# Attention over a long context on one core: value products of two key tiles one behind the other in every second step

## The chip, the cores and the metric

One core of one Trainium2 chip runs the whole program. The metric is the device time of one execution in microseconds (us), the median of three executions of the kernel before: 3383.43 us.

## The reference, cut to what matters

`x` is 32 examples of 64 latent rows of width 256; `ctx_512` is 32 examples of 1601 context rows of width 64. Six blocks are added to `x` one after the other: a small cross attention, a self attention, a quantised MLP, then the cross attention over the whole context (the block that the change touches), a self attention and a mixture of experts.

```
q_big = rope((hidden_q @ Wq.T) per head @ w_kc_q)        # 16 heads, width 192
kv_r  = rope(kv_c)                                       # 1601 x 64, shared by the heads
q_r   = einsum('bshq,hqr->bhsr', q_big, W_qr)
k_r   = einsum('bld,hdr->bhlr', kv_r, W_kr)
scores = einsum('bhsr,bhlr->bhsl', q_r, k_r)
attn  = softmax(scores, axis=-1)
ctx_c = einsum('bhsl,bld->bhsd', attn, kv_r)
out   = einsum('bhsd,hkd->bhsk', ctx_c, w_kc_kv) ... @ Wo.T
```

## The kernel before

The block is `context_attention`. The per-head weights have been folded ahead of it, so that for every example (a **batch** here, n = 0 to 31) the scores are products of the turned context keys with 1024 query columns (16 heads of 64 rows), held as two halves p = 0, 1 of 512 columns. Two batches share one tile of 128 rows of `x`: the even one (e = 0) comes first, then the odd one (e = 1). The 16 tiles are the repeats of the work; most of them run in a loop over t.

The 1601 keys lie in NKT = 13 tiles of 128 (the last has 65). A batch has 13 **steps**, kt = 0 to 12. The order on each engine is written out by hand in its `batch` function, and semaphores tie the engines together. In step kt:

- TensorE (PE in the profile) makes the scores of the *next* key tile, `scores(n, t, e, kt + 1, p)` (L813 and L814, two products that are added, into the PSUM banks `st[0]` and `st[1]`), one half in each of the first two thirds of the step. In the last third it makes the value products of *this* key tile, `values(n, e, kt)` (L825): the 128x64 tile of `kv` against the 512 exponentials of each half, the halves into partitions 0 to 63 and 64 to 127 of the one bank `av`, where all 13 key tiles are summed. The trace shows the two products of a `values` as four matmuls.
- ScalarE (ACT) makes the exponentials, `exps(n, kt)` (L965): one of 128x512 for each half, from `st[p]` into `prob`, a ring of RING = 4 buffers, and a fifth for key tile 12. A buffer is free again once the value products and the sum over keys (POOL) of four tiles before are done.
- GpSimd (POOL) adds the exponentials up over the key tiles, `add(n, kt)` (L685).
- VectorE (DVE) takes row maxima of the *next* batch: TensorE makes 16 **pieces** of plain scores a batch (`max_scores`, L790, into the two `mx` banks in turn), VectorE reduces each (`reduce_max`, L1062). A piece's products wait until VectorE is through with the piece two before it. The function `pieces` spreads the 16 over the thirds: in an even batch from the second third of step 1 to the end of step 6, in an odd one from step 3 to step 9.

`scores(kt + 2, p)` needs `st[p]` back, so it waits for the exponential of kt + 1, half p. `values(kt)` waits for both exponentials of kt, and in step 0 for `summed` (ScalarE's copy of the last batch's `av`). Other work lies on TensorE between the thirds:

- after step 0 `denominators(n - 1)` (L837), once GpSimd's last addition of the batch before is done; later, in steps 2 and 3, VectorE inverts them in two halves (`invert`, L1075) and scales the heads (L1080), in its program behind the pieces of step 2 and of step 3;
- after step 5 of an even batch `out(t - 1)` (L844), after step 6 `turn_x` (L737), which waits for all 16 pieces;
- in steps 7 to 12 of an even batch the queries of the next tile (L747, L761); in steps 7 to 10 of every batch the turning of keys (L728);
- in step 11 `max_rows` (L799), 16 small products, which ScalarE copies before the next batch's first scores can start; they stand ahead of that step's value products.

The lines that set the order of scores and values are these:

```
for kt in range(NKT):
    for third in range(3):
        if third == 2:
            values(n, e, kt)
        elif kt + 1 < NKT:
            scores(n, t, e, kt + 1, third)
```

Of the kernel before, what the change touches and what calls it, by code (L numbers as in the profile page):

```python
# [403 lines left out]
NKT = -(-SK // P)  # L404
# [77 lines left out]
def context_attention(nc, sb, pb, sem, a, x_all, const, wbig, mw, wvo):  # L482
# [91 lines left out]
    def nk(kt):  # L574
        return min(P, SK - kt * P)
# [13 lines left out]
    def pieces(e, kt, third):  # L589

        start, end = (9, 3 * NEGATE_AT + 3) if e else (4, 3 * QUERIES_AT)
        first = lambda k: min(max(0, -(-(k - start) * PIECES // (end - start))), PIECES)
        return range(first(3 * kt + third), first(3 * kt + third + 1))

    def slot(kt):

        return kt % RING if kt < NKT - 1 else RING
# [13 lines left out]
    def is_first(n):  # L611
        return isinstance(n, int) and n == 0

    with nc.Block() as block:
# [105 lines left out]
        def _(pe):  # L720
            def turn_keys(n, r):

                if r == 0:
                    pe.wait_ge(s_kl, n + 1)
                else:
                    pe.wait_ge(s_kp, KROUNDS * n + r)
                for kt in range(4 * r, min(4 * r + 4, NKT)):
                    last = pe.transpose(misc[:, kt % 4 * P:(kt % 4 + 1) * P], khl[:, kt, :, :], ident[:, :])  # L728
                last.then_inc(s_kt, 1)

            def turn_x(t):
                pe.wait_ge(s_xn, t + 1)

                if not is_first(t):
                    pe.wait_ge(s_mr, 2 * t * PIECES)
                for c in range(DC):
                    last = pe.transpose(mx[0][:, 0, c * P:(c + 1) * P], xn[:, c * P:(c + 1) * P], ident[:, :])  # L737
                last.then_inc(s_xT, 1)
# [27 lines left out]
            def queries(t, j):  # L766

                if 2 <= j < CP + 2:
                    effective(t, j - 2)
                if j < CP:  # L770
                    big(t, j)

            def max_scores(t, n, e, i):
                b = i % 2
                if i == 0:

                    pe.wait_ge(s_kp, KROUNDS * (n + 1))
                    if e == 0:
                        pe.wait_ge(s_q1a, 2 * t + 2)
                        pe.wait_ge(s_q2a, 2 * t + 2)  # L780
                    else:
                        pe.wait_ge(s_q1b, t + 1)
                        pe.wait_ge(s_q2b, t + 1)
                if not (is_first(n) and i < 2):

                    pe.wait_ge(s_mr, n * PIECES + max(i - 1, 0))
                q = q1[e][:, :, :, :].rearrange("p e j s -> p (e j s)")[:, (i // 2) * P:(i // 2 + 1) * P]
                for h in range(2):
                    lo = (2 * b + h) * KQ
                    last = pe.matmul(mx[b][:, h, 0:KQ], q, kp[e][:, lo:lo + KQ], start=True, stop=True)  # L790
                last.then_inc(s_mx, 1)

            def max_rows(n, p):

                if p == 0:
                    pe.wait_ge(s_nm, n + 1)
                for i in range(4):
                    for part, (w, lo) in enumerate(((nmh, True), (nml, False))):
                        last = pe.matmul(mx[p][0:1, 0, i * P:(i + 1) * P], w[:, 4 * p + i:4 * p + i + 1], identb[:, :],  # L799
                                         start=(part == 0), stop=(part == 1))  # L800
                last.then_inc(s_row, 1)

            def scores(n, t, e, kt, p):
                keys = slice(kt * P, kt * P + nk(kt))
                g = 2 * kt + p
                if not (is_first(n) and g < 2):

                    pe.wait_ge(s_exp, n * 2 * NKT + g - 1)
                if g == 0:

                    pe.wait_ge(s_rowk, 2 * n + 2)
                    pe.wait_ge(s_kd[e], 32 * t + 32)
                pe.matmul(st[p][0:nk(kt), :], k1[e][:, keys], q1[e][:, p, :, :], start=True, stop=False)  # L813
                pe.matmul(st[p][0:nk(kt), :], k2[e][:, keys], q2[e][:, p, :, :], start=False, stop=True)\  # L814
                    .then_inc(s_st, 1)

            def values(n, e, kt):
                pe.wait_ge(s_exp, n * 2 * NKT + 2 * kt + 2)
                if kt == 0:

                    pe.wait_ge(s_kv, n + 1)
                    if not is_first(n):
                        pe.wait_ge(s_avk, n)
                for p in range(2):
                    last = pe.matmul(av[DCX * p:DCX * p + DCX, :], kv[e][0:nk(kt), kt, :],  # L825
                                     prob[slot(kt)][0:nk(kt), p, :], start=(kt == 0), stop=(kt == NKT - 1))
                last.then_inc(s_av, 1)

            def denominators(n):

                pe.wait_ge(s_acc, (n + 1) * NSUM)
                if isinstance(n, int) and n > 0:

                    pe.wait_ge(*((s_hd, n) if n % 2 else (s_x, n // 2)))
                pe.wait_ge(s_rowk, min(2 * n + 4, 2 * B) if isinstance(n, int) else 2 * n + 4)
                for p in range(2):
                    last = pe.matmul(misc[DCX * p:DCX * p + DCX, :], ones[:, :], acc[:, p, :], start=True, stop=True)  # L837
                last.then_inc(s_sum, 1)

            def out(t):  # L840

                pe.wait_ge(s_hd, 2 * t + 2)
                for j in range(CP):
                    last = pe.matmul(misc[:, 0:D], heads[:, j, :, :], wvo[:, j, :],  # L844
                                     start=(j == 0), stop=(j == CP - 1))
                last.then_inc(s_out, 1)
# [18 lines left out]
            def batch(n, t, e, more, next, far):  # L865
                for kt in range(NKT):
                    for third in range(3):
                        if third == 2:
                            values(n, e, kt)
                        elif kt + 1 < NKT:  # L870
                            scores(n, t, e, kt + 1, third)
                        elif next:
                            scores(n + 1, t + e, 1 - e, 0, third)
                        if more and e == 0 and third < 2 and 0 <= kt - QUERIES_AT <= CP // 2:
                            queries(t + 1, 2 * (kt - QUERIES_AT) + third)
                        if next:
                            for i in pieces(e, kt, third):
                                max_scores(t + e, n + 1, 1 - e, i)
                            if kt == ROWS_AT and third == 1:
                                max_rows(n + 1, 0)  # L880
                                max_rows(n + 1, 1)
                    if kt == QUERIES_AT - 1 and more and e == 0:
                        turn_x(t + 1)
                    if kt == 0 and not is_first(n):
                        denominators(n - 1)
                    if kt == OUT_AT and e == 0 and not is_first(n):
                        out(t - 1)
                    if 0 <= kt - TURN_AT < KROUNDS and more:
                        if kt == TURN_AT and not is_first(n):

                            if e == 0:
                                pe.wait_ge(s_x, t)
                            else:
                                pe.wait_ge(s_hd, n)
                        turn_keys(n + 2, kt - TURN_AT)

            batches(pe, before, batch)
            denominators(B - 1)
            out(NT - 1)
# [990 lines left out]
```

## Time and profile before

| what | value |
|---|---|
| median of 3 executions | 3383.43 us (3383.25 to 3397.73) |
| profiled execution, its own time | 3396.48 us |
| its span | 3394.7 us |
| mean granted TensorE clock over the span | 0.928 of full speed |
| busy TensorE / VectorE / ScalarE / GpSimd | 86% / 47% / 37% / 36% of the span |

The span is what lies between the first and the last instruction on the core. The profiled execution is one of several, and it took 13 us more than the median. The context attention runs from about 757 us to 2530 us of the span. Busy TensorE means that a matmul was in flight, at either clock.

### The profile page before, as it was taken

The numbers are of one execution on the slowest core, as the hardware profiler recorded it, in microseconds if no ns is written. First come the engines' busy times: TensorE is split into PE (matmuls) and PEld (weight loads), VectorE is DVE, ScalarE is ACT, GpSimd is POOL, SyncE is SP. The second block draws the span as 40 slices with busy tenths as digits, with TensorE's granted clock in tenths as the row PEclk, the third lists the DMA queues.
The fourth block names the chain that finished last, engine by engine and source line by source line (L and its number), as shares of the span: only waits on it lengthen the run. The fifth ranks groups of instructions, "written<-read, shape, count | busy, mean of one in ns | idle before, by whom it ended". The sixth has DMA issues, their size and how long they took to land. (4 is left out here: it accounts for less than half of the span.)

```text
span 3394.7 us, 49700 instructions
## 1 busy us (share of the span) xinstructions
PE 2916.8 (86%) x17527; PEld 1787.8 (53%) x17528; DVE 1579.7 (47%) x2705; ACT 1260.5 (37%) x2514; POOL 1232.9 (36%) x656
## 2 busy tenths in 40 slices
PE   5867734659999999999999999999977789999998
PEld 3544422535545554555455554555434467777776
DVE  3444567533554455444544464445526643333232
ACT  3433412114344334433443344344424333333332
POOL 0000000035676567656765676557650000000000
PEclk9778866679999999999999999999988899999999
DMA  1000030011111011110111111111011000000000
GB/s 40 0 17 0 0 121 0 0 58 40 36 49 39 25 35 49 39 35 33 41 39 35 39 35 39 35 39 35 30 72 77 0 1 0 0 0 0 0 0 25
DMA packets 26434, 98.27 MB, mean 29 GB/s; under 512 B 3536, under 2 KB 8272, under 8 KB 24976
## 3 DMA queue, kind: packets, MB, share of 16 engines
q1 hardware_dynamic: 24720, 94.02, 8.4%
q10 hardware_dynamic: 1664, 3.58, 0.3%
q8 instruction: 32, 0.52, 0.1%
q14 instruction: 18, 0.15, 0.0%
HBM read 55.97 MB, written 2.10 MB: 17 GB/s over the span
## 5 line engine op out<-in xcount | busy, mean ns | idle before, releaser
L685 POOL TENSOR_TENSOR cx_acc<-cx_acc,cx_prob 128x1024 f32<-128x1024 f32 (+1 forms) x352 | 834.7, 2371 | 509.0 <-ACT cx_prob L965 501.5
L965 ACT ACTIVATE cx_prob<-cx_st 128x512 f32<-128x512 f32 (+1 forms) x832 | 477.5, 596 | 595.2 <-PE cx_st L814 577.5
L1062 DVE TENSOR_REDUCE cx_mhalf<-cx_mx 128x1 f32<-128x804 f32 x512 | 486.1, 988 | 219.2 <-PE cx_mx L790 219.1
L825 PE MATMUL cx_av<-cx_prob,cx_kv 128*64 128x512 f32 (+1 forms) x1664 | 456.8, 628 | 0.0
L813 PE MATMUL cx_st<-cx_q,cx_k 128*128 128x512 f32 (+1 forms) x832 | 369.0, 444 | 50.0 <-ACT cx_prob L965 49.4
L1528 PE MATMUL moe_gu<-moe_wgu,moe_xnT 128*128 128x352 f32 x1280 | 397.6, 462 | 0.0
L790 PE MATMUL cx_mx<-cx_kp,cx_q 128*128 128x402 f32 x1024 | 304.0, 380 | 62.6 <-DVE cx_mhalf L1062 59.2
L814 PE MATMUL cx_st<-cx_q,cx_k 128*128 128x512 f32 (+1 forms) x832 | 332.4, 400 | 0.0
L1528 PEld LDWEIGHTS moe_gu<-moe_wgu,moe_xnT 128*128 128x128 f32 x1280 | 241.5, 191 | 124.1 <-issue 6.2
L790 PEld LDWEIGHTS cx_mx<-cx_kp,cx_q 128*128 128x128 f32 x1024 | 174.7, 193 | 248.5 <-DVE cx_mhalf L1062 186.0
L1043 DVE TENSOR_TENSOR cx_turn<-cx_mx,cx_tab 128x384 f32<-128x384 f32 x256 | 130.9, 553 | 358.3 <-PE cx_mx L747 358.3
L1663 DVE SCALAR_TENSOR_TENSOR moe_hid<-moe_silu,moe_coef,moe_gu 128x176 f32<-128x176 f32 x320 | 127.0, 397 | 350.2 <-ACT moe_silu L1591 348.1
L813 PEld LDWEIGHTS cx_st<-cx_q,cx_k 128*128 128x128 f32 (+1 forms) x832 | 157.8, 190 | 204.2 <-ACT cx_prob L965 143.7
L1591 ACT ACTIVATE moe_silu<-moe_gu 128x176 f32<-128x176 f32 x320 | 101.6, 318 | 370.8 <-PE moe_gu L1528 370.8
L1493 POOL TENSOR_TENSOR moe_rstd<-moe_mv,minus_half 128x1 f32<-128x1 f32 x16 | 8.8, 549 | 614.2 <-DVE moe_mv L1628 614.2
L1551 PE MATMUL moe_acc<-moe_wd,moe_hidT 128*128 128x256 f32 (+1 forms) x896 | 216.1, 382 | 0.0
L747 PE MATMUL cx_mx<-cx_xnT,cx_wbig 128*128 128x128 f32 x1536 | 204.7, 283 | 0.5 <-ACT cx_xnT L928 0.5
L761 PE MATMUL cx_mx<-cx_turn,cx_mw 128*64 128x128 f32 (+1 forms) x2048 | 197.0, 296 | 0.0
L747 PEld LDWEIGHTS cx_mx<-cx_xnT,cx_wbig 128*128 128x128 f32 x1536 | 183.2, 192 | 25.0 <-issue 16.5
L924 ACT CAST cx_kp<-cx_misc 128x512 fp32r<-128x512 f32 (+1 forms) x128 | 64.8, 507 | 324.2 <-PE cx_misc L728 324.2
L1551 PEld LDWEIGHTS moe_acc<-moe_wd,moe_hidT 128*128 128x128 f32 (+1 forms) x896 | 160.2, 190 | 21.9 <-issue 5.3
L814 PEld LDWEIGHTS cx_st<-cx_q,cx_k 128*128 128x128 f32 (+1 forms) x832 | 156.8, 188 | 7.5
(209 smaller groups left out, 3701.3 us busy)
## 6 DMA issues: line engine op xcount, KB each, us to landing
cx_k<-cx_kp SPq DMA_DIRECT2D x32, 804.0 KB, 4.0
cx_ctx<-in_cx_ctxN SPq DMA_DIRECT2D x32, 416.0 KB, 3.2
cx_ctxr<-in_cx_ctxrN SPq DMA_DIRECT2D x32, 416.0 KB, 3.9
cx_k<-cx_kp SPq DMA_DIRECT2D x32, 402.0 KB, 5.2
moe_wgu<-in_moe_wgu SPq DMA_DIRECT2D x5, 1408.0 KB, 14.6
moe_wd<-in_moe_wd SPq DMA_DIRECT2D x4, 896.0 KB, 24.6
x_all<-in_x SPq DMA_DIRECT2D x1, 2048.0 KB, 4.2
cx_wq<-in_cx_wq SPq DMA_DIRECT2D x1, 2048.0 KB, 11.8
```

What stands on the lines that cost most here:

```text
L685: pool.tensor_tensor(acc[rows, :, :], sofar, prob[slot(kt)][rows, :, :], ALU.add).then_inc(s_acc, 1)
L747: last = pe.matmul(mx[j % 2][:, 0, tile * P:(tile + 1) * P], wbig[:, c, j, tile * P:(tile + 1) * P], xnT[:, c, :], start=(c == 0), stop=(c ...
L761: last = pe.matmul(mx[j // 4][DCX * e:DCX * e + DCX, 1, at:at + P], mw[rows, j, cs, tile, :], turn[j % 2][rows, cs, tile, :, :], start=(cs ...
L790: last = pe.matmul(mx[b][:, h, 0:KQ], q, kp[e][:, lo:lo + KQ], start=True, stop=True)
L813: pe.matmul(st[p][0:nk(kt), :], k1[e][:, keys], q1[e][:, p, :, :], start=True, stop=False)
L814: pe.matmul(st[p][0:nk(kt), :], k2[e][:, keys], q2[e][:, p, :, :], start=False, stop=True)\
L825: last = pe.matmul(av[DCX * p:DCX * p + DCX, :], kv[e][0:nk(kt), kt, :], prob[slot(kt)][0:nk(kt), p, :], start=(kt == 0), stop=(kt == NKT ...
L965: act.activation(prob[slot(kt)][rows, p, :], st[p][rows, :], ACT.Exp).then_inc(s_exp, 1)
L1043: last = dve.tensor_tensor(turn[j % 2][:, cs, :, :, :], q, tab[:, cs, :, :].unsqueeze(2).broadcast_to([P, 3, 2, S]), ALU.mult)
L1062: dve.tensor_reduce(mhalf[:, i // 2, i % 2:i % 2 + 1], mx[i % 2][:, :, 0:KQ], AX.XY, ALU.max)\
L1528: last = pe.matmul(gu[i][:, 0:2 * FE], xnT[g][:, c, :], wgu[:, e, c, :], start=(c == 0), stop=(c == DC - 1))
L1551: last = pe.matmul(acc[:, 0:D], hidT[q % 2][0:n, k % 4, :], wd[0:n, k, :], start=(k == 0), stop=(k == NFC - 1))
```

## The change

`values` is no longer made in steps 0, 2, 4, 6, 8 and 10. In each odd step the value products of the key tile before and of this one stand one behind the other; step 12, the last, makes those of key tile 12 alone, as before. No product is added or left out; scores, pieces and all else stay where they were.

```
                 for kt in range(NKT):
                     for third in range(3):
                         if third == 2:
-                            values(n, e, kt)
+                            if kt % 2 == 1:
+                                values(n, e, kt - 1)
+                            if kt % 2 == 1 or kt == NKT - 1:
+                                values(n, e, kt)
                         elif kt + 1 < NKT:
                             scores(n, t, e, kt + 1, third)
```

TensorE, the start of an odd batch in the loop (steps 0 and 1; REGISTER_ALU and ISA rows compute addresses and waits). Before:

```order
L825 MATMUL cx_av<-cx_prob,cx_kv 64x512 x2
L831 REGISTER_ALU
L835 ISA
L837 MATMUL cx_misc<-cx_acc,cx_ones 64x512 x2
L808 REGISTER_ALU
L813 MATMUL cx_st<-cx_q,cx_k 128x512
L814 MATMUL cx_st<-cx_q,cx_k 128x512
L808 REGISTER_ALU
L813 MATMUL cx_st<-cx_q,cx_k 128x512
L814 MATMUL cx_st<-cx_q,cx_k 128x512
L825 MATMUL cx_av<-cx_prob,cx_kv 64x512 x2
```

With the change:

```order
L831 REGISTER_ALU
L835 ISA
L837 MATMUL cx_misc<-cx_acc,cx_ones 64x512 x2
L808 REGISTER_ALU
L813 MATMUL cx_st<-cx_q,cx_k 128x512
L814 MATMUL cx_st<-cx_q,cx_k 128x512
L808 REGISTER_ALU
L813 MATMUL cx_st<-cx_q,cx_k 128x512
L814 MATMUL cx_st<-cx_q,cx_k 128x512
L821 REGISTER_ALU
L825 MATMUL cx_av<-cx_prob,cx_kv 64x512 x4
```

The value products of key tile 0 have left their place ahead of the denominators (L837) and stand with those of key tile 1, behind the scores of key tile 2.

TensorE, even batch, the end of step 4 and the start of step 5 (the pieces are the L790 rows). Before:

```order
L813 MATMUL cx_st<-cx_q,cx_k 128x512
L814 MATMUL cx_st<-cx_q,cx_k 128x512
L786 REGISTER_ALU
L790 MATMUL cx_mx<-cx_kp,cx_q 128x402 x2
L825 MATMUL cx_av<-cx_prob,cx_kv 64x512 x2
L786 REGISTER_ALU
L790 MATMUL cx_mx<-cx_kp,cx_q 128x402 x2
```

With the change:

```order
L813 MATMUL cx_st<-cx_q,cx_k 128x512
L814 MATMUL cx_st<-cx_q,cx_k 128x512
L786 REGISTER_ALU
L790 MATMUL cx_mx<-cx_kp,cx_q 128x402 x2
L786 REGISTER_ALU
L790 MATMUL cx_mx<-cx_kp,cx_q 128x402 x2
```

The two pieces now follow each other directly; the value products that stood between them come behind the pieces of step 5.

## Rows read from the trace of the kernel before

**Rows 1.** Windows: the context attention, then one tile slow in clock, one not
```profile
core 0: us, PE busy (x) PEld busy (x) DVE busy (x) ACT busy (x) POOL busy (x), PEclk, DMA share, GB/s
757.00:2530.00 1773.00, 1642.49 (x9019) 921.68 (x9018) 865.50 (x1096) 738.27 (x1341) 1143.24 (x516) 0.98 0.11 36
...
1392.06:1504.14 112.08, 104.35 (x582) 58.91 (x581) 55.78 (x71) 46.67 (x86) 72.71 (x34) 0.98 0.11 37
1504.14:1614.69 110.55, 102.84 (x581) 58.23 (x580) 55.78 (x71) 46.67 (x86) 72.69 (x34) 1.00 0.12 38
```

**Rows 2.** Waits of TensorE, 800 to 2480 us: total, times, longest
```profile
PE cx_mx L790 <- DVE cx_mhalf L1062: 53.7, 45, 1.7
PE cx_st L813 <- ACT cx_prob L965: 48.7, 61, 1.8
```

**Rows 3.** The page's part 5, exponentials and reductions: busy, mean ns, idle before
```profile
L965 ACT ACTIVATE cx_prob<-cx_st 128x512 f32<-128x512 f32 (+1 forms) x832 | 477.5, 596 | 595.2 <-PE cx_st L814 577.5
L1062 DVE TENSOR_REDUCE cx_mhalf<-cx_mx 128x1 f32<-128x804 f32 x512 | 486.1, 988 | 219.2 <-PE cx_mx L790 219.1
```

**Rows 4.** Timeline of TensorE around one value step: start, us, [idle before]
```profile
1415.32 0.53 PE L790 MATMUL cx_mx<-cx_kp,cx_q 128*128 128x402 f32 x2
1415.69 0.39 PE L813 MATMUL cx_st<-cx_q,cx_k 128*128 128x512 f32 x1
...
1416.15 0.53 PE L790 MATMUL cx_mx<-cx_kp,cx_q 128*128 128x402 f32 x2
1416.60 1.08 PE L825 MATMUL cx_av<-cx_prob,cx_kv 128*64 128x512 f32 x4
1417.61 0.64 PE L790 MATMUL cx_mx<-cx_kp,cx_q 128*128 128x402 f32 x2
1418.09 0.39 PE L813 MATMUL cx_st<-cx_q,cx_k 128*128 128x512 f32 x1
```

**Rows 5.** Timeline of TensorE, odd batch, steps 0 to 2
```profile
1506.27 1.08 PE L825 MATMUL cx_av<-cx_prob,cx_kv 128*64 128x512 f32 x4
1507.18 1.03 PE L837 MATMUL cx_misc<-cx_acc,cx_ones 128*64 128x512 f32 x4
1508.68 0.50 PE L813 MATMUL cx_st<-cx_q,cx_k 128*128 128x512 f32 x1 [0.47 <-ACT cx_prob L965]
...
1509.83 1.08 PE L825 MATMUL cx_av<-cx_prob,cx_kv 128*64 128x512 f32 x4
1512.72 0.50 PE L813 MATMUL cx_st<-cx_q,cx_k 128*128 128x512 f32 x1 [1.81 <-ACT cx_prob L965]
```

**Rows 6.** Timeline of TensorE, even batch, steps 4 to 6
```profile
1452.40 1.08 PE L825 MATMUL cx_av<-cx_prob,cx_kv 128*64 128x512 f32 x4
1455.14 0.64 PE L790 MATMUL cx_mx<-cx_kp,cx_q 128*128 128x402 f32 x2 [1.66 <-DVE cx_mhalf L1062]
...
1458.99 3.61 PE L844 MATMUL cx_misc<-cx_wvo,cx_heads 128*128 128x256 f32 x16
...
1465.42 0.44 PE L737 MATMUL cx_mx<-ident,cx_xn 128*128 128x128 f32 x2 [0.16 <-DVE cx_mhalf L1062]
```

**Rows 7.** Timeline of TensorE, odd batch, steps 4 and 5
```profile
1519.62 1.08 PE L825 MATMUL cx_av<-cx_prob,cx_kv 128*64 128x512 f32 x4
...
1522.78 0.64 PE L790 MATMUL cx_mx<-cx_kp,cx_q 128*128 128x402 f32 x2 [1.05 <-DVE cx_mhalf L1062]
```

**Rows 8.** Timeline of VectorE in the same steps of that batch
```profile
1519.34 1.76 DVE L1075 RECIPROCAL cx_misc<-cx_misc 128x256 f32<-128x256 f32 x1
1521.13 0.69 DVE L1080 TENSOR_TENSOR cx_heads<-cx_summed,cx_misc 128x512 f32<-128x512 f32 x1
```

**Rows 9.** Timeline of TensorE, where the even batch begins
```profile
1434.29 0.50 PE L813 MATMUL cx_st<-cx_q,cx_k 128*128 128x512 f32 x1 [0.48 <-ACT cx_prob L965]
...
1439.02 1.08 PE L837 MATMUL cx_misc<-cx_acc,cx_ones 128*64 128x512 f32 x4 [0.38 <-POOL cx_acc L685]
```

**Rows 10.** Windows: the same work of an odd batch in two tiles
```profile
1401.80:1405.34 3.54, 3.54 (x10) 1.75 (x10) 0.07 (x1) 1.07 (x3) 3.46 (x2) 0.52 0.00 0
1513.88:1515.83 1.95, 1.95 (x10) 1.05 (x10) 0.07 (x1) 0.85 (x3) 1.87 (x2) 1.00 0.00 0
```

## The prediction

> **What bounds the kernel now.** I read the windows first, then the waits, then the timelines of one tile, engine by engine. The change touches 757 to 2530 us alone. There TensorE is busy for 1642 of 1773 us, GpSimd for 1143, VectorE for 866, ScalarE for 738 [rows 1]: TensorE sets the time wherever it doesn't wait. The tiles repeat: of the 14 in the middle, 11 take 112.1 us at a granted clock of 0.98 and three take 110.5 us at 1.00. TensorE's waits are few and always in the same places: 53.7 us for VectorE ahead of pieces, 48.7 us for ScalarE ahead of scores [rows 2]. These places decide. A value product that leaves a step where TensorE then waits leaves for nothing, since the wait grows by as much; where it lands, it costs its full time.
>
> **What the change saves.** The value products use the array in two halves of 64 columns (the form 128\*64), all around them uses it whole (128\*128). Each change of form shows in the starts [rows 4]: from a piece to the scores behind it 0.37 us; from a piece to value products 0.45; from value products to the next piece 1.01, where from value products to denominators, of the same form, it is 0.91 [rows 5]; and the first piece behind value products takes 0.48 instead of 0.37. So a visit to the narrow form costs 0.08 + 0.10 + 0.10 = about 0.28 us of TensorE besides the 0.91 us of its work. A batch loses five visits (steps 2, 4, 6, 8, 10; in step 0 the denominators keep the form), 160 in all, and at most 160 x 0.28 = 45 us.
>
> The page "TensorEngine Tiling (Array Packing)" of the Trainium skill, section on tiling modes, says that changing the mode drains the array; by this rule alone the sum would be those 45 us, with no price for the waits. The rows agree that a change costs something.
>
> **What it costs, step by step.** I move the value products in the timelines with the durations above: 0.91 us for a second `values` behind a first, 0.60 us for an exponential, about 0.95 to 0.99 us for a reduction [rows 3]. V4 stands for the value products of key tile 4.
>
> *Even batch.*
> - V0: TensorE waits 0.38 us for GpSimd's last addition ahead of the denominators [rows 9]. Without V0 that wait is 1.3 us; V0 lands in step 1: **+0.91**.
> - V2: VectorE falls behind. It needs three reductions (2.9 us) a step, TensorE's step without values gives only 0.93 for scores and 1.1 for pieces, so its pieces wait 0.9 us; what is left of the gain is given back when V2 lands: **about 0**, with VectorE's chain through both reciprocals 0.9 us late from V0.
> - V4: the wait of 1.66 us ahead of the first piece behind it [rows 6] is VectorE's (reciprocal, heads, reduction). V4's leaving makes it 2.6 to 2.9 us; its landing in step 5 delays `out`: **+0.91**.
> - V6: `turn_x` waits 0.16 us for the last reductions [rows 6], which end when they end; V6 lands in step 7, where queries keep TensorE full: **+0.91**.
> - V8: full TensorE on both sides: **-0.28**.
> - V10: full ahead, and behind step 11 stands a wait of 0.48 us for ScalarE's chain from `max_rows` to the exponential [rows 9], which V10 now fills: -0.28 - 0.5, **about -0.8**.
>
> Sum: 3 x 0.91 - 0.28 - 0.8 = about +1.6 us; drawn through the timelines I get +1.5.
>
> *Odd batch.*
> - V0: ScalarE holds the scores of step 1 (0.47 us of wait) and of step 2 (1.81) [rows 5]: V0 leaves one wait and fills half of the other: **0**, and the 1.81 becomes 0.9.
> - V2: without V2 the scores of key tile 4 wait for the exponential of 3 (score to score at least 0.9 + 0.6 us): leaves 0.6 to 0.7, lands 0.91, a switch less: **about +0.2**.
> - V4: the first piece of step 5 waits 1.05 us for VectorE's second reciprocal (1.76 us), the heads (0.69) and a reduction [rows 7, 8]. The wait becomes 2.2 us, V4 lands behind it: **+0.8**.
> - V6, V8: two pieces a step leave VectorE time. V6 gains its 0.28 and loses it to a piece's wait, V8 gains 0.28 and takes up a wait for keys: **-0.3** together.
> - V10: as in the even batch, but TensorE stands idle sooner, for the exponentials: **-0.2**; and what has become late is partly hidden where the next batch waits for GpSimd's additions: **-0.2**.
>
> Sum: about +0.3 us. A tile therefore gains 1.5 + 0.25 = +1.75 us; over 15 tiles with pieces **+26 us**. The ends: if each landing costs only 0.6 us (part of the new waits vanishing, as V2's), a tile is at 5 x 0.6 less 2.5 saved, or 0; if the savings of steps 8 and 10 don't come, it is at +3.3, or 50 us. Scalar and vector work, DMAs and GpSimd's additions are the same and keep their order. The ring of exponentials doesn't bind: exponential 4 waits for V0, now in step 1, and is asked for at the end of step 3.
>
> **The clock.** In 11 of the 14 tiles TensorE's clock falls from 2.4 to 1.2 GHz right behind the wait of 1.81 us, and never behind those of 1.66 or 1.05 us. The same work then takes 3.54 us instead of 1.95 [rows 10], and the tile 1.55 us more [rows 1]. The change takes this wait to 0.9 us: 11 x 1.55 = 17 us saved if the dips go. It makes two longer ones, 2.6 to 2.9 us (even, step 5) and 2.2 us (odd, step 5). If each brings the dip as often as the 1.81 did, with 1.2 us of it on the path since VectorE is behind there anyway, that is 2 x 11 x 1.2 = 26 us more. Net +9; with dips in every tile at both places 15 x 2 x 1.3 - 17 = +22; with none -17. I take **+12**.
>
> The page "TensorE: Matmul & The Clock Gate" of the Trainium skill (its table on why this matters) warns against idle gaps between bursts of matmuls, since they bring the clock back to half; by this rule the two new waits speak against the change, and the sum with that term is +38 us, without it +26. The trace agrees for the wait of 1.81 us.
>
> **Sum.** +26 + 12 = +38 us. The profiled execution took 3396.5 us and would take 3434; it stands 13 us above the median, perhaps by its dips, and I lay the sum on the median: 3383.4 + 38 = **3421 us**.
>
> **Rivals.**
> - *The switches are worth it (faster).* The waits on VectorE and ScalarE don't grow, because what TensorE does earlier brings the pieces and scores earlier by as much: the mechanism is the mode change, its place every even step, its price 0.28 us, and it decides once fewer than two of the five landings a tile cost their 0.91. With all 160: 3383 - 45 = 3338 us. With the landings at half price (5 x 0.45 = 2.3 us) and ten visits at 0.28 (2.8 us): -0.5 us a tile, and the clock's -17: about 3359 us. For it: TensorE is 93% busy. Against: all five landings leave a place that shows a wait [rows 5 to 7, 9]. Chance 0.10.
> - *A draw.* The landings cost as I say, but more of it is hidden at batch ends by ScalarE and GpSimd, and the clock dips fall away without new ones: 26 - 17 + little = 3383 to 3400 us. Chance 0.22.
> - *VectorE's bound in full.* Every even step with pieces loses 0.9 us against VectorE's reductions, and both new waits bring a dip in every tile: 50 + 22 = +72, 3455 us. For it: reductions take 2.9 us where TensorE's work for the same pieces now takes 2.0. Against: the paired products leave VectorE 2 us to catch up, and the odd batch has only two pieces in most steps. Chance 0.15.
> - *Nothing changes in kind:* the trace of after would show the same waits. It can't be: the order of instructions differs as shown. Chance 0.
>
> My forecast (3400 to 3445 us) has 0.53.
>
> **How the numbers follow.** 0.5% is 17 us, about what can be told from no change here. Slower by more, over 3400: the forecast and the third rival, 0.68. Faster by more, under 3366: 0.10. Within: 0.22. The range for 8 in 10 reaches down over the draw, to 3380, and up to 3452, short of the third rival's end.
>
> **What would show it.** In the new profile: value products in runs of eight matmuls, the second four 0.91 us behind the first; 160 fewer changes of form; the wait at the denominators of the even batch at 1.3 us; the wait in step 5 of the even batch above 2.4 us and that of the odd one at 2.2; the 1.81 us wait at 0.9 and no dip behind it; dips behind the two in step 5; tile periods of 113 to 116 us. I am wrong if the tile period falls below 110.5 us, if the waits for VectorE stay near 54 us in sum, or if the clock stays at 1.00 in most tiles.

## The result and the profile after

| | before | with the change |
|---|---|---|
| median | 3384.62 us (3383.25 to 3397.73, 4 runs) | 3454.18 us (3439.20 to 3459.22, 4 runs) |
| profiled execution, its span | 3396.48, 3394.7 us | 3459.22, 3457.4 us |
| mean granted TensorE clock | 0.928 | 0.917 |

The change made the kernel slower: the ratio is 1.0189, with a 95% interval of 1.0158 to 1.0220. The direction and the places were as forecast, but the loss was larger: the medians differ by 70 us, the means of the executions (from which the ratio comes) by 64, where I had said 38. The median of 3454 us lies above my forecast of 3400 to 3445 us, and 2 us above the 3452 to which the range for 8 in 10 reached; 1.0189 of the 3383.4 us on which I had laid the sum is 3447.

Busy time in the profile of the change (part 1 of the page), and its costliest groups that the change touches (part 5). The lines below `values` have moved by three (L965 is L968, L1062 is L1065).

```profile
PE 2920.2 (84%) x17527; PEld 1824.7 (53%) x17528; DVE 1597.9 (46%) x2705; ACT 1259.2 (36%) x2514; POOL 1230.2 (36%) x656
...
L825 PE MATMUL cx_av<-cx_prob,cx_kv 128*64 128x512 f32 (+1 forms) x1664 | 425.0, 630 | 0.0
L790 PE MATMUL cx_mx<-cx_kp,cx_q 128*128 128x402 f32 x1024 | 319.5, 397 | 89.7 <-DVE cx_mhalf L1065 86.2
```

The instruction counts are the same, and TensorE is busy for as long as before (2920 us against 2917) in a span that is 63 us longer. The value products themselves (L825) are busy for 425 us instead of 457, for less of each visit is overhead. The pieces (L790) have become longer one by one (397 ns against 380). A slower clock would do that: the rows below show a piece at 1.04 us instead of 0.64.

The waits of TensorE in the context attention of the change, 800 to 2540 us, to be read as [rows 2]: total, times, longest.

```profile
PE cx_mx L790 <- DVE cx_mhalf L1065: 80.8, 60, 2.7
PE cx_st L813 <- ACT cx_prob L968: 44.1, 60, 1.3
PE cx_misc L837 <- POOL cx_acc L685: 26.6, 14, 1.9
PE cx_mx L737 <- DVE cx_mhalf L1065: 17.6, 15, 1.3
```

The wait for VectorE ahead of pieces has grown from 53.7 to 80.8 us, and two waits that were small are now large: for GpSimd ahead of the denominators (0.38 us each before [rows 9], now 1.9) and for VectorE ahead of `turn_x` (0.16 before [rows 6], now 1.2). The longest wait for ScalarE has gone from 1.81 us [rows 5] to 1.3.

Timeline of TensorE in the change, an even batch: the denominators, the first pair of value products, the long wait for VectorE and what follows it, and `turn_x`.

```profile
1581.90 1.08 PE L837 MATMUL cx_misc<-cx_acc,cx_ones 128*64 128x512 f32 x4 [1.91 <-POOL cx_acc L685]
...
1584.40 1.94 PE L825 MATMUL cx_av<-cx_prob,cx_kv 128*64 128x512 f32 x8
1586.27 0.64 PE L790 MATMUL cx_mx<-cx_kp,cx_q 128*128 128x402 f32 x2
...
1598.31 1.04 PE L790 MATMUL cx_mx<-cx_kp,cx_q 128*128 128x402 f32 x2 [2.67 <-DVE cx_mhalf L1065]
...
1602.33 3.01 PE L825 MATMUL cx_av<-cx_prob,cx_kv 128*64 128x512 f32 x8
...
1612.20 0.44 PE L737 MATMUL cx_mx<-ident,cx_xn 128*128 128x128 f32 x2 [1.16 <-DVE cx_mhalf L1065]
```

Two `values` take 1.87 us from their start to that of the piece behind them, where one takes 1.01 [rows 4], so the second costs 0.86 us. At 1598.31 TensorE has waited 2.67 us for VectorE, where before it was 1.66 [rows 6]. Behind that wait a piece takes 1.04 us instead of 0.64 and the eight value products 3.01 instead of 1.94. This is the clock at 1.2 GHz. The windows of that stretch, of the stretch behind the long wait of an odd batch, and of one even and two odd batches of the change (each from the value products of key tile 12 to those of the next batch) show the granted clock in the sixth group of numbers:

```profile
1598.31:1605.27 6.96, 6.96 (x19) 3.92 (x19) 3.84 (x4) 1.97 (x3) 2.38 (x2) 0.55 0.21 85
1669.59:1674.29 4.70, 4.70 (x15) 2.41 (x15) 2.84 (x3) 1.37 (x2) 3.80 (x2) 0.66 0.52 181
...
1535.42:1577.79 42.37, 36.75 (x170) 19.57 (x170) 27.79 (x31) 24.00 (x48) 33.92 (x17) 1.00 0.13 45
1577.79:1650.70 72.91, 66.91 (x413) 41.36 (x412) 29.30 (x40) 22.59 (x39) 38.65 (x18) 0.95 0.10 31
1650.70:1694.45 43.75, 38.12 (x171) 20.52 (x170) 27.99 (x31) 24.01 (x48) 33.92 (x17) 0.96 0.13 44
```

The same batches before took 68.73 us (even) and 41.77 us (odd, without a dip) at a clock of 1.00:

```profile
1435.41:1504.14 68.73, 65.17 (x413) 39.13 (x412) 29.01 (x40) 22.54 (x39) 37.90 (x18) 1.00 0.12 35
1504.14:1545.91 41.77, 37.61 (x171) 19.10 (x170) 26.77 (x31) 24.14 (x48) 34.84 (x17) 1.00 0.12 43
```

So a tile, an odd and an even batch, went from 112.1 or 110.5 us to 115.3 or 116.8; over the 14 in the middle the mean is 116.05 us, against 111.74 before.

Not every even batch of the change is like the one shown. In six of the 14 in the middle the clock falls once, behind the 2.67 us, and the low clock lasts as in the window from 1598.31. In seven it falls twice: behind the wait of 1.9 us for GpSimd ahead of the denominators, and, for a shorter time, behind the 2.67 us. The remaining one has a single, shorter dip (71.27 us). Here is one of the seven, its wait at the denominators, and the windows of the whole batch and of the stretches behind its two waits:

```profile
1698.53 1.08 PE L837 MATMUL cx_misc<-cx_acc,cx_ones 128*64 128x512 f32 x4 [1.89 <-POOL cx_acc L685]
```

```profile
1694.45:1767.54 73.09, 67.08 (x413) 41.23 (x412) 29.17 (x40) 22.70 (x39) 38.57 (x18) 0.95 0.10 31
1698.53:1705.00 6.47, 6.47 (x21) 2.87 (x22) 1.94 (x2) 2.70 (x5) 4.71 (x2) 0.74 0.00 0
1716.52:1722.00 5.48, 5.48 (x18) 3.16 (x18) 3.74 (x4) 1.97 (x3) 1.75 (x2) 0.69 0.27 106
```

What of the loss is the order and what is the clock, the experiments had to tell. A stretch in which the granted clock is at the lower of its two levels, 1.2 GHz, is called a **dip** in what follows.

### The profile page after: what moved, and what is told of

The parts are those of the page before. It is cut to its first block and busy times, and to the rows that moved or that the text cites. A ratio compares the mean times of both kernels' runs of the same rounds, so it can differ in the third digit from the quotient of the medians.

```text
span 3457.4 us, 49700 instructions
## 1 busy us (share of the span) xinstructions
PE 2920.2 (84%) x17527; PEld 1824.7 (53%) x17528; DVE 1597.9 (46%) x2705; ACT 1259.2 (36%) x2514; POOL 1230.2 (36%) x656
## 5 line engine op out<-in xcount | busy, mean ns | idle before, releaser
L968 ACT ACTIVATE cx_prob<-cx_st 128x512 f32<-128x512 f32 (+1 forms) x832 | 477.6, 596 | 672.4 <-PE cx_st L814 638.5
L1065 DVE TENSOR_REDUCE cx_mhalf<-cx_mx 128x1 f32<-128x804 f32 x512 | 485.8, 988 | 277.8 <-PE cx_mx L790 277.8
L825 PE MATMUL cx_av<-cx_prob,cx_kv 128*64 128x512 f32 (+1 forms) x1664 | 425.0, 630 | 0.0
L813 PE MATMUL cx_st<-cx_q,cx_k 128*128 128x512 f32 (+1 forms) x832 | 374.5, 450 | 47.8 <-ACT cx_prob L968 47.0
L790 PE MATMUL cx_mx<-cx_kp,cx_q 128*128 128x402 f32 x1024 | 319.5, 397 | 89.7 <-DVE cx_mhalf L1065 86.2
L814 PE MATMUL cx_st<-cx_q,cx_k 128*128 128x512 f32 (+1 forms) x832 | 339.9, 409 | 0.0
L790 PEld LDWEIGHTS cx_mx<-cx_kp,cx_q 128*128 128x128 f32 x1024 | 189.5, 207 | 235.5 <-DVE cx_mhalf L1065 188.1
L813 PEld LDWEIGHTS cx_st<-cx_q,cx_k 128*128 128x128 f32 (+1 forms) x832 | 158.5, 191 | 192.1 <-ACT cx_prob L968 140.0
L825 PEld LDWEIGHTS cx_av<-cx_prob,cx_kv 128*64 128x64 f32 (+1 forms) x1664 | 104.4, 143 | 184.1 <-issue 153.7
```

The lines of the kernel that those rows point to most:

```text
L968: act.activation(prob[slot(kt)][rows, p, :], st[p][rows, :], ACT.Exp).then_inc(s_exp, 1)
L1065: dve.tensor_reduce(mhalf[:, i // 2, i % 2:i % 2 + 1], mx[i % 2][:, :, 0:KQ], AX.XY, ALU.max)\
```

## The experiments

The kernels are built on the kernel before. In its `batch` on TensorE the key tiles in `LATE` have their value products put off to the next step; the first tuple is for even batches, the second for odd ones. With `(0, 2, 4, 6, 8, 10)` in both this is the change itself.

```
+    LATE = ((0, 2, 4, 6, 8, 10), (0, 2, 4, 6, 8, 10))
...
                         if third == 2:
-                            values(n, e, kt)
+                            if kt - 1 in LATE[e]:
+                                values(n, e, kt - 1)
+                            if kt not in LATE[e]:
+                                values(n, e, kt)
```

In what follows "a batch takes" means from the value products of its predecessor's key tile 12 to those of its own. The line numbers of these kernels stand one above those of the change (`max_scores` is L791, `values` L826).

### The change with its two longest waits filled

```
+            def fill(n, e, p):
+                pe.wait_ge(s_exp, n * 2 * NKT + 11 + p)
+                for _ in range(7):
+                    pe.matmul(st[p][:, :], k1[e][:, 0:P], q1[e][:, p, :, :], start=True, stop=True)
...
+                        if (e, kt, third) in ((0, 4, 2), (1, 5, 0)):
+                            fill(n, e, e)
                         if next:
                             for i in pieces(e, kt, third):
```

The seven products go to the bank that the next scores overwrite, after the exponential has read it. They add work on TensorE; no other engine reads what they write.

> The changed kernel with seven matmuls of 128x512 added in each batch (products whose result is overwritten unread), in the wait for VectorE in step 5 (even: ahead of the last piece of step 4; odd: ahead of the first piece of step 5). They add work and take none away. Theory A (the clock): in the trace of the change the granted clock falls behind these two waits (2.67 us, 2.2 us), for 6.8 us in every even batch and for 3.4 us in every second odd one; that costs about 2.7 us and 1.4 us, some 50 us in all. With TensorE busy in the waits the dips go: even batch (end of its last value products to the end of the next) from 72.9 to about 70.2 us, the whole 1.007 to 1.010 of before. Theory B (the landings of value products behind VectorE's waits are all of it, the clock comes along for nothing): even batch stays at 72.9 us, the whole at 1.019 of before.

Measured: 3409.37 us median (6 runs), 1.0066 of before, interval 1.0040 to 1.0093. Timeline of TensorE in step 4 and 5 of an even batch, and the windows of an even and an odd batch:

```profile
1451.81 1.79 PE L834 MATMUL cx_st<-cx_q,cx_k 128*128 128x512 f32 x7
1454.64 0.63 PE L791 MATMUL cx_mx<-cx_kp,cx_q 128*128 128x402 f32 x2 [1.04 <-DVE cx_mhalf L1074]
```

```profile
1434.16:1504.27 70.11, 65.74 (x419) 40.84 (x418) 28.98 (x40) 22.59 (x39) 38.69 (x18) 1.00 0.11 32
1504.27:1546.66 42.39, 38.47 (x177) 20.79 (x176) 27.79 (x31) 24.00 (x48) 33.99 (x17) 1.00 0.13 45
```

Seven matmuls of useless work (L834) in every batch made the changed kernel 45 us faster by the medians, 52 by the profiled executions. The piece behind the wait starts when VectorE lets it, as in the change, but it takes 0.63 us instead of 1.04. The even batch falls from 72.9 to 70.1 us, the odd one stays at 42.4 and is no longer 43.75 in every second tile. Theory A holds and B falls, though 1.0066 lies a little below the 1.007 to 1.010 expected. Four of the 14 even batches in the middle still dip, now behind the 1.9 us at the denominators, and take 71.6 to 73.1 us. The 6.8 us of low clock "in every even batch" of my expectation is true of six of the 14. This run also splits the loss: at full clock the order alone costs 70.1 - 68.7 = 1.4 us in an even batch and 42.4 - 41.8 = 0.6 us in an odd one, 2.0 us a tile or 30 us over 15 tiles. The rest is put down to the clock.

### Key tile 4 alone

`LATE = ((4,), (4,))`.

> Only the value products of key tile 4 are put off to step 5, in every batch. Theory A (value products that leave a wait cost their full time where they land, plus the clock behind the longer wait): even batch +0.9 us and a dip of 1.4 to 2.7 us, odd batch +0.8 us and a dip in half of the tiles: a tile 112.1 us becomes about 115.5, the whole 1.013 to 1.018 of before. Theory B (each of the five put off value products costs a like share of the loss): about a fifth of 70 us, 1.004 of before.

Measured: 3434.67 us (4 runs), 1.0144, interval 1.0113 to 1.0174. Windows of an even batch with and of one without a dip, and of an odd one without:

```profile
1439.22:1511.47 72.25, 67.66 (x413) 41.02 (x412) 29.29 (x40) 22.55 (x39) 37.83 (x18) 0.95 0.11 33
...
1555.41:1625.01 69.60, 65.00 (x412) 39.21 (x411) 29.02 (x40) 22.53 (x39) 37.87 (x18) 1.00 0.11 34
1625.01:1667.66 42.65, 37.31 (x170) 19.19 (x169) 26.76 (x31) 24.11 (x48) 34.81 (x17) 1.00 0.12 42
```

Without a dip V4 costs 69.6 - 68.75 = 0.86 us in the even batch and 0.87 in the odd one: the full time of the second of a pair. The saved change of form goes into the wait, which has grown by 1.01 us, from 1.66 to 2.67. Nine of the 14 even batches in the middle have a dip, and with it V4 costs up to 3.5 us. One of the six put off value products, alone, makes three quarters of the slowdown. An equal share (theory B) would have been a fifth.

### All but key tile 4

`LATE = ((0, 2, 6, 8, 10), (0, 2, 6, 8, 10))`.

> The change with the value products of key tile 4 left in step 4 (0, 2, 6, 8 and 10 are put off). Theory A: the two long waits in step 5 keep V4 ahead of them and stay near 1.7 and 1.1 us, so nearly all dips of the change go (about 3.5 us a tile) and V4's landings with them (1.7 us): a tile of 116 us becomes about 111, the whole 1.003 to 1.006 of before. Theory B (each of the five put off is a like share): four fifths of the loss, 1.015.

Measured: 3398.86 us (8 runs), 1.0034, interval 1.0016 to 1.0053. Two waits in the timeline of an even batch, and the windows of an even and an odd batch:

```profile
1431.22 1.97 PE L838 MATMUL cx_misc<-cx_acc,cx_ones 128*64 128x512 f32 x4 [1.92 <-POOL cx_acc L686]
...
1449.16 0.64 PE L791 MATMUL cx_mx<-cx_kp,cx_q 128*128 128x402 f32 x2 [1.66 <-DVE cx_mhalf L1066]
```

```profile
1427.11:1497.96 70.85, 65.83 (x413) 40.08 (x412) 29.03 (x40) 22.60 (x39) 38.66 (x18) 0.98 0.11 32
1497.96:1539.49 41.53, 37.04 (x171) 19.50 (x170) 27.79 (x31) 24.00 (x48) 33.97 (x17) 1.00 0.14 46
```

The wait ahead of step 5 is back at 1.66 us and the piece behind it is quick. But the dips didn't go, as I had expected them to. All 14 even batches in the middle have one behind the wait for GpSimd ahead of the denominators (1.92 us), which then take 1.97 us instead of 1.08, where in the change it was seven of 14; two have a second behind the 1.66 us. The dips in the odd batches are gone. A tile takes 112.4 us. The ratio is in the range that I gave, the tile time above the 111 us that A gave.

### Key tiles 0 and 6 of the even batches

`LATE = ((0, 6), ())`.

> Only the value products of key tiles 0 and 6 of the even batches are put off by a step. Both leave a wait (0.38 us for GpSimd ahead of the denominators, 0.16 us for VectorE ahead of turn_x) that grows instead, and both land where TensorE is full. Theory A: 0.86 us each where they land (the second of a pair in the trace of the change), less what hides it: even batch 68.75 to about 70.2 us, and where the wait of 1.3 us ahead of the denominators lets the clock fall, some 0.2 us more: 1.006 to 1.008 of before. Theory B (the changes of form are saved, the waits stay as they are): 68.2 us, 0.998.

Measured: 3419.02 us (6 runs), 1.0093, interval 1.0066 to 1.0120. Windows of an even batch with and of one without a dip (an odd one without a dip takes 41.77 us, as before):

```profile
1437.81:1509.87 72.06, 66.50 (x413) 39.94 (x412) 28.99 (x40) 22.66 (x39) 37.80 (x18) 0.98 0.11 33
...
1553.19:1623.64 70.45, 64.91 (x413) 39.33 (x412) 29.00 (x40) 22.54 (x39) 37.84 (x18) 1.00 0.11 34
```

Two landings cost 70.45 - 68.75 = 1.70 us, 0.85 each. Theory B falls. Three of the 14 even batches in the middle have a dip behind the wait at the denominators (1.37 us), and it costs 1.6 us, not 0.2. The ratio lies above my 1.006 to 1.008, though its interval reaches into that range.

### Key tile 2 alone

`LATE = ((2,), (2,))`.

> Only the value products of key tile 2 are put off to step 3, in every batch. My term for it was about 0 in the even and +0.2 us in the odd batch: a tile within 0.5 us of before, ratio 1.000 to 1.004. If V2 costs like V4 (0.9 us in each batch) the ratio is 1.007 or more.

Measured: 3371.02 us (6 runs), 0.9947, interval 0.9927 to 0.9966, faster than I had said. Windows of an odd and an even batch:

```profile
1378.11:1420.17 42.06, 37.53 (x171) 19.15 (x170) 26.78 (x31) 24.14 (x48) 34.84 (x17) 1.00 0.12 43
1420.17:1488.32 68.15, 65.19 (x412) 39.12 (x412) 28.92 (x40) 22.54 (x39) 37.88 (x18) 1.00 0.12 35
```

The odd batch loses 0.29 us (I had 0.2), but the even one gains 0.6 (I had 0). V2 leaves a place where TensorE now waits only 0.27 us for VectorE, so most of its time is won there, and it lands ahead of the wait of 0.87 us that TensorE had for VectorE at the start of step 4. That wait is gone in this kernel, and the one of 1.66 us is as before. I had drawn V2 together with V0, whose landing made that chain late, and had not seen that V2 alone is a gain. A tile gains 0.3 us, 5 us in all, and there are 8 dips instead of 11 in the profiled execution, 5 us more. That is less than the 18 us of the ratio, or the 24.5 us between the two profiled executions. Of the latter 11 us lie ahead of the context attention, in code that the edit doesn't touch: its first scores begin at 758.9 us of the span, in the kernel before at 770.0. So the batches explain the sign and about 10 us; the rest isn't shown to be the edit's.

### Key tile 0 of the odd batches

`LATE = ((), (0,))`.

> Only the value products of key tile 0 of the odd batches are put off to step 1, where scores then wait 1.81 us for ScalarE. Theory A: they fit into that wait, it becomes 0.94 us, nothing else is later, and the clock no longer dips behind it: no tile at 112.1 us, all at 110.5, 3379 us by the profile where before took 3396; against before's median, whose executions differ in the number of dips, 0.995 to 1.000. Theory B (the order costs time wherever the value products go later): 1.002 or more. Theory C (the dips come from something else than this wait): tiles still at 112.1 us, ratio 1.000.

Measured: 3374.72 us (12 runs), 0.9952, interval 0.9934 to 0.9970; the profiled execution took 3375.45 us. Windows of an odd batch and an even one:

```profile
1499.12:1540.85 41.73, 37.60 (x170) 19.10 (x170) 26.77 (x31) 24.10 (x48) 34.81 (x17) 1.00 0.12 43
1540.85:1609.61 68.76, 65.18 (x413) 39.15 (x412) 29.01 (x40) 22.54 (x39) 37.87 (x18) 1.00 0.12 35
```

At full clock nothing is saved: the batches take what they took. But every odd batch of the profiled execution now takes 41.7 us, and none 43.3. Ten of the eleven dips in the 14 tiles before stood behind the wait of 1.81 us, and all ten are gone; theories B and C fall. One dip is left, in an even batch behind the wait of 1.66 us (70.20 us instead of 68.75). The kernel before has such a one too, in the last of its 14 tiles.

### Key tiles 8 and 10

`LATE = ((8, 10), (10,))`.

> Only the value products of key tiles 8 and 10 of the even batches and of key tile 10 of the odd ones are put off by a step, where TensorE has no wait ahead of it. Theory A: a visit to the narrow form less is worth 0.28 us each, and that of 10 moves into the wait of 0.48 us for ScalarE behind step 11: even batch 68.7 to about 67.7 us, odd batch 41.8 to about 41.3, some 1.4 us a tile, the whole 0.993 to 0.995 of before. Theory B (no gain from fewer changes of form, a wait takes it up): 1.000.

Measured: 3367.94 us (9 runs), 0.9940, interval 0.9917 to 0.9963.

```profile
1493.80:1535.19 41.39, 37.47 (x171) 19.14 (x170) 26.79 (x31) 23.99 (x48) 34.12 (x17) 1.00 0.13 45
1535.19:1603.18 67.99, 64.54 (x413) 39.25 (x412) 29.01 (x40) 22.59 (x39) 38.57 (x18) 1.00 0.11 34
```

The even batch gains 0.75 us, the odd one 0.37, and the ratio is in the range of theory A. Busy TensorE shrinks by 0.63 us in the even batch (65.17 to 64.54), two changes of form at 0.3. The half microsecond that V10 should have gained in the wait behind step 11 is mostly taken back at the denominators: GpSimd's additions set their time, and the wait for them grew from 0.38 us to 0.76. The dips have moved as well: three of the 14 odd batches in the middle have one behind the 1.81 us instead of ten, and four of the even ones behind the 1.66 us instead of one.

### The other parity

`LATE = ((1, 3, 5, 7, 9, 11), (1, 3, 5, 7, 9, 11))`.

> The same pairing with the other parity: value products of key tiles 1, 3, 5, 7, 9 and 11 are put off to the even step behind, six visits to the narrow form less a batch, as many as the change. Theory A (what counts is the wait that each leaves and lands in): V3 now lands in the waits of 1.66 and 1.05 us for VectorE, so these shrink below 1 us and bring no dip; V5, V7, V9 save 0.28 each; V1 of the odd batch leaves the wait of 1.81 us, which becomes about 3 us with a dip in every tile, V11 leaves the wait of 0.48 us, which becomes 1.7; both cost about 0.9 where they land. A tile is at -1.5 to +1.0 us without the clock and up to +2.5 with it: 0.995 to 1.011 of before, and faster than the change by about 1%. Theory B (two value products in a row are bad whatever the step, since VectorE and ScalarE starve meanwhile): as the change, 1.015 to 1.02.

Measured: 3437.07 us (4 runs), 1.0151, interval 1.0117 to 1.0184. That is 0.4% less than the change and not 1%, with intervals that overlap, and it is outside the range that I gave for theory A. The number lies just inside that of theory B. The timeline of TensorE shows why, first in an odd batch, then in the even one behind it, then in the next even one, where the clock stays up in these steps:

```profile
1415.99 0.51 PE L814 MATMUL cx_st<-cx_q,cx_k 128*128 128x512 f32 x1 [2.81 <-ACT cx_prob L969]
...
1466.61 0.64 PE L791 MATMUL cx_mx<-cx_kp,cx_q 128*128 128x402 f32 x2 [1.88 <-DVE cx_mhalf L1066]
...
1469.80 2.59 PE L826 MATMUL cx_av<-cx_prob,cx_kv 128*64 128x512 f32 x8
1472.32 0.64 PE L791 MATMUL cx_mx<-cx_kp,cx_q 128*128 128x402 f32 x2
...
1581.81 0.63 PE L791 MATMUL cx_mx<-cx_kp,cx_q 128*128 128x402 f32 x2 [1.88 <-DVE cx_mhalf L1066]
...
1586.90 0.63 PE L791 MATMUL cx_mx<-cx_kp,cx_q 128*128 128x402 f32 x2 [0.79 <-DVE cx_mhalf L1066]
```

Windows of two odd batches and of an even one, here from first scores to first scores (before: 41.74 us for an odd and 68.75 for an even batch at full clock):

```profile
1405.46:1449.98 44.52, 38.14 (x169) 20.00 (x170) 25.75 (x31) 24.06 (x48) 34.63 (x17) 0.96 0.11 36
...
1519.55:1565.20 45.65, 39.24 (x170) 20.52 (x170) 25.75 (x31) 24.06 (x48) 34.63 (x17) 0.93 0.11 36
1565.20:1634.19 68.99, 64.05 (x412) 39.53 (x412) 28.93 (x41) 22.53 (x39) 37.93 (x17) 1.00 0.12 37
```

V1 and V11 left waits, which became 2.81 and 1.5 us as expected. V3 did what A said of it: the wait of 1.66 us behind step 4 of the even batch [rows 6] is down to 0.79 us (1586.90), or gone where the matmuls ahead of it run slow (1472.32), and the one of 1.05 us in the odd batch is down to 0.20. What A had left out is the place that V3 leaves. Ahead of step 4 of the even batch stood a wait of 0.87 us for VectorE, behind the first of its two reciprocals, and this is the one that is now 1.88 us (1466.61, 1581.81). The wait for turned keys in the odd batch grew from 0.35 us to about 1.2. In sum the even batch loses 0.24 us at full clock. The odd batch loses 2.8 or 3.9 us, and it has a dip behind the 2.81 us in every tile; in every second tile the even batch has one too, behind the 1.88 us. A tile takes 114.1 or 114.6 us. No odd batch is without a dip, so the clock's part of this wasn't separated. The time alone would speak for B; against B as a rule stand the even batch here, and the kernels with V8, V10 or V2 put off, where two value products in a row gain.

### The useful ones together, twice

`LATE = ((8, 10), (0, 10))`, and then `((8, 10), (0, 8, 10))`.

> Only the useful ones: put off are V8 and V10 in the even batches, V0 and V10 in the odd ones. Theory A (the terms add): even 68.0 us, odd 41.4, no dip in most tiles, a tile at 109.4 us against 110.5 or 112.1: 0.989 to 0.993 of before. Theory B (V0 and V10 share one gain, the wait at the batch's start): 0.994 or more, no better than either alone.

> As the one before with V8 of the odd batches put off too. It leaves step 8, where no wait is near, and lands in step 9 behind two pieces. Theory A: 0.28 us a tile less, odd batch 41.1 us, 0.001 below the one before. Theory B (VectorE's two pieces in step 8 or the keys' turning take it up): the same time as the one before.

Measured: 3351.11 us (6 runs), 0.9897, interval 0.9870 to 0.9924, and 3346.17 us (6 runs), 0.9899, interval 0.9872 to 0.9927. Windows of an even and an odd batch of the first kernel, then an odd and an even one of the second:

```profile
1427.36:1495.33 67.97, 64.55 (x412) 39.25 (x411) 28.99 (x40) 22.61 (x39) 38.52 (x18) 1.00 0.11 34
1495.33:1536.77 41.44, 37.49 (x171) 19.14 (x170) 26.78 (x31) 24.03 (x48) 34.18 (x17) 1.00 0.13 45
```

```profile
1476.19:1517.42 41.23, 37.20 (x170) 19.32 (x170) 27.87 (x31) 24.01 (x48) 33.96 (x17) 1.00 0.13 46
1517.42:1585.54 68.12, 64.53 (x412) 39.25 (x411) 29.08 (x40) 22.58 (x39) 38.67 (x18) 1.00 0.11 33
```

The first is at 109.4 us a tile, what I had forecast for it, at full clock in 13 of the 14 tiles in the middle: theory A holds. V8 of the odd batches makes the odd batch 0.2 us shorter and the even one 0.15 longer, so the two kernels can't be told apart, which was theory B for the second. Both beat the kernel before by 1.0% and the change by 2.9%. About half of the 1.0% is the order (109.4 us against 110.5), about half the dips that are gone. V2 of the even batches, found later, was not tried together with them.

## Why the prediction was right, and where it was short

**The direction and its reason** were right: a value product that leaves a wait leaves for nothing and costs its full time where it lands. The forecasts of the waits came out: 2.6 to 2.9 us in step 5 of the even batch (2.67), 2.2 in the odd one (2.20), 0.9 in place of 1.81 (0.94). The one at the denominators was mis-sized: 1.3 us foretold, 1.9 found. V0 alone accounts for what I had foretold (1.37 us in the kernel with V0 and V6 put off). The rest is GpSimd's last addition, which comes later with V8 and V10 put off: in the kernel with these alone the wait is 0.76 us instead of 0.38.

**The term of the order**, +26 us, was nearly right: 1.4 + 0.6 us a tile, 30 us. Its parts, from the batches at full clock:

| part | forecast | measured |
|---|---|---|
| V0 and V6, even | +1.8 us | +1.70 |
| V4, even / odd | +0.91 / +0.8 | +0.86 / +0.87 |
| V2, even / odd | 0 / +0.2 | -0.6 / +0.29 |
| V8 and V10, even | -1.1 | -0.75 |
| V10, odd, with what the next batch hides | -0.4 | -0.37 |
| V0, odd | 0 | 0 |
| both batches, all six | +1.75 | +2.0 |

The -0.75 and the -0.37 are from one kernel, and what V10 of the odd batch does to the start of the next even one is in the first of them. V6 of the odd batch wasn't run alone; V8 of it, in the last two kernels, is -0.2 us in the odd batch and +0.15 in the next. The two larger errors in the even batch work against each other, which is luck: V2 gains 0.6 us where I had 0, and V8 and V10 save 0.35 less than I had. The even parts add up to +1.2 us, where the filled kernel has 1.4. Two slips in the working change nothing: where it says that a tile gains 1.75 us it gets longer by as much, and the lower end, 5 x 0.6 less 2.5, is 0.5 us and not 0.

**The term of the clock**, +12 us, is the step that failed. It had the right sign and was less than half of what the runs show. Three things in it were wrong.

- The reading of the kernel before. I wrote that the clock never falls behind the wait of 1.66 us. Of the 11 slow tiles, ten have their dip behind the 1.81 us; the eleventh has it in the even batch, behind the 1.66 us:

```profile
2347.16 0.90 PE L790 MATMUL cx_mx<-cx_kp,cx_q 128*128 128x402 f32 x2 [1.66 <-DVE cx_mhalf L1062]
```

- The price and the number of dips. I took 1.2 us for a dip, since VectorE would be behind anyway, and a dip in 11 of 14 tiles at each of the two places. The even batch of the change takes 72.98 us on average (14 in the middle), and 70.13 at full clock in the filled kernel: 2.8 us for the clock, with a dip in every one. Every second odd batch dips behind the 2.2 us, at 43.75 - 42.38 = 1.4 us.
- A place that I had put at nothing: the wait at the denominators, 1.9 us, behind which seven of the 14 even batches have the first of their two dips.

Per tile this is 2.8 + 0.7 = 3.5 us in place of my 2 x 0.79 x 1.2 = 1.9. Less the 1.2 us that the old dips cost on average (11 of 14 tiles at 1.55), the clock gives +2.3 us a tile, 32 to 34 us over 14 or 15 tiles. With the 30 us of the order that is 62 to 64 us; the two profiled executions differ by 62.7, the means by 64.

**The rivals.** The first (the switches are worth it) fell as a whole, but is true of single places: V8 and V10 gain, and so does V2 in the even batch. The second (a draw) fell with its condition, that no new dips come. The third (VectorE's bound in full, 3455 us) came close to the time by luck: it had 50 us for the order, where 30 were found, and 22 for the clock, where 32 were, and it asked for a dip in every tile at both new waits, which only the even batch has.

**The pages.** The page "TensorEngine Tiling (Array Packing)" of the Trainium skill, section on tiling modes, says that a change of mode drains the array, and gives no price. The trace agrees that a change costs something: two visits less took 0.63 us from TensorE's busy time in the even batch. The page "TensorE: Matmul & The Clock Gate" of the Trainium skill, in its table "Why this matters for your kernels", warns of idle gaps between bursts of matmuls because they bring the clock down. Its warning is for gaps longer than any that I applied it to, so by the page alone neither the 1.81 us nor the two new waits would have counted; the prediction should have said so. The measurement decides: in these traces the clock fell behind waits of 1.37 to 2.81 us. Without the term of the clock the forecast would have been 3409 us, 45 us short of the median.

## What to carry to other kernels

Before moving work on the bound engine, mark its waits. In this kernel work that stood ahead of a wait was free there and cost its full time anywhere else, and work moved into a wait without touching what ends it was free from then on. Look at both ends of a move: with the other parity I had counted the wait that V3 fills and not the one that it leaves. Count the clock as part of the price of a wait on TensorE: the waits of 1.9 and 2.7 us of an even batch cost 2.8 us more in slow matmuls behind them, so that filling one with useless products paid. Try the parts of a regular change one by one: in the even batches V2 gained, and V8 and V10 together; V4 lost, and V0 and V6 together. The sum hid both.

## What the runs showed that I had not expected

- The length of a wait doesn't tell by itself whether the clock falls behind it. Of the 14 batches in the middle that have it, the wait of 1.81 us brought a dip in ten before, in seven with key tile 2 put off and in three with 8 and 10; the one of 1.66 us in one before and in four with 8 and 10. The one of 1.9 us at the denominators brought it in seven in the change, in four in the filled kernel and in all 14 with key tile 4 left in place. In the filled kernel nothing was done at that wait. What else decides, these runs don't show.
- The kernel before does not have one time. In 20 executions beside the first four experiments it took 3375.91 to 3399.51 us. The dips in the context attention needn't be the reason. The two last kernels, profiled, take 3363.91 and 3343.03 us, 21 us apart, with one dip each in their middle 14 tiles and 1705 us from the first scores to the last value products in both. What differs lies ahead of the block, where the code is the same: 775.0 us in one and 755.8 in the other, with a granted clock of 0.75 and 0.77. That difference of 19 us is as large as what several of the edits do, so a profiled execution is best compared by its batches and not by its whole.

```profile
0.00:775.00 775.00, 492.52 (x4164) 314.03 (x4164) 394.47 (x794) 225.03 (x461) 71.28 (x106) 0.75 0.08 27
0.00:755.80 755.80, 471.31 (x4164) 300.32 (x4164) 394.23 (x794) 224.75 (x461) 71.23 (x106) 0.77 0.08 27
```
